# A three-stage fp32 kernel on one core: another order of instructions at the opening, at the entry of the value phase and in the last pair, and five more products on zeros

## The chip, the cores and the metric

The kernel runs on one core of a Trainium2 chip. The metric is the device time of one execution in microseconds (us); smaller is better. The engines of a core run side by side and meet at semaphores: TensorE (PE) multiplies, VectorE (DVE), ScalarE (ACT) and GpSimd (POOL) do the element-wise work, SyncE (SP) issues the DMAs.

## The reference

1024 tokens of width 512 pass through three blocks, each with a layer normalisation in front and a residual around it:

```python
x = x + 0.5 * ffn(layernorm(x))      # ffn: scores = xf @ Wr.T; top 16 of 64 experts, softmax gates G
x = x +       attn(layernorm(x))     #      h = xf @ A (64 experts of rank 16); out = (h * G) @ B * 2
x = x + 0.5 * ffn(layernorm(x))      # attn: q, k, v of 32 heads of 128, causal over 256 tokens, then wo
```

All of it is fp32. The mixture of low-rank experts is dense: up to 64 + 1024 columns for each token (the router's scores and all experts' h), gates that are zero for 48 experts, and down from 1024 to 512.

## The kernel before, in words

Every fp32 product is made of three products of a rounded part (hi) and a rest (lo): `mm3`, lines 226 to 229, whose instructions the profile shows as L227, L228 and L229. So whatever TensorE multiplies must first be split: one engine makes hi by a copy (ScalarE, L499), another makes lo by a subtraction (VectorE, L741 or L1523; GpSimd, L1291, L1073, L1014).

Tokens are worked on in 8 tiles of 128. For one tile the first feed-forward does this: VectorE takes mean and variance (`dve_stats`, L746, L748), GpSimd the reciprocal root (`pool_rstd`, L1005, L1008), VectorE normalises into `xn` (`dve_normalise`, L754), TensorE transposes xn in four pieces (`pe_ffn_transpose`, L235), ScalarE and VectorE split it into `xT_hi` and `xT_lo` (`act_ffn_transposed`, `dve_ffn_transposed`), TensorE multiplies by the up weights in three chunks of 384, 384 and 320 columns over four k (`pe_ffn_up`, PSUM banks `ub`), VectorE finds the top 16 and the gates (`dve_route`, L815 to L822) and writes the gated hidden values `hg` in three pieces (L830), TensorE transposes them in eight pieces (`pe_ffn_gated_transpose`, L268), they are split into `hT_hi` and `hT_lo`, TensorE multiplies by the down weights in 24 products of 512 columns (`pe_ffn_down`, bank `fb`), and VectorE adds the result to x (`dve_combine`, L845). TensorE's written order interleaves the tiles: gated transposes of t-1, up of t, transposes of t+1, down of t-1. `xT_hi` and `xT_lo` exist once.

For the first tile the order is by k, not by chunk (`pe_ffn_up_first`, L238), because the four slices of the up weights arrive by DMA one after the other and are split as they arrive (ScalarE L1440, VectorE L1523). Ahead of it stand ten products on zeros (L1342). GpSimd makes `downT_lo` in four subtractions (L1291) after the reciprocal root of tile 1 and ahead of that of tile 2.

The value phase makes v for all heads by a Strassen-like scheme with seven products per group and four groups: `pe_v(g, i, c)` is product i for column tile c of 128 tokens, six matrix instructions of 512 columns each. Its weights pass through a ring of three: ScalarE writes hi (`act_v_weight`), GpSimd the rest (`pool_v_weight`, L1073). Its inputs are the attention's normalised tokens `xa`, transposed (`pe_att_transpose`, L292), for tiles 4 to 7 with seven steps on VectorE that form the sums `comb_raw` (`dve_att_transposed_half1`, L779 to L791, counted by `comb_step`), a rounded copy on ScalarE (`act_combined`) and the rest on VectorE (`dve_combined`, counted by `comb_split`). The entry to this phase is interleaved with the last tiles of the feed-forward, lines 1370 to 1390 on TensorE.

Then come 16 pairs of heads. `pe_pair` has four steps j for a pair; step j holds products for the next pair's q and k, output products of earlier attention (`pe_output(p, t)`: tile t of x gets the pair's contribution, six instructions of 512 columns; VectorE adds it to x in `dve_output`, L939), transposes of the probabilities (`pe_prob_transpose`, L423), the scores of the next step (`pe_scores`, from L413) and the attended values (`pe_attend`, L441). Between scores and the next transposes lie VectorE's row maximum (L858), ScalarE's exponentials (L544), VectorE's reciprocal and scaling (L866, L870); between the transposes and the scores that overwrite their bank lie ScalarE's copies and VectorE's `pT_lo`. In the last pair (`final=True`) there are no q and k products of a next pair. After it come the transposes of the first tile of the second feed-forward, which is like the first, and the output products 2 to 7 of the last pair (lines 1414 to 1418).

All order is written out by hand, engine by engine; each engine works strictly in its written order and waits on semaphores. DMAs are issued by SyncE alone, in one queue.

## Time and profile before

| | us |
|---|---|
| median of 3 runs | 1074.53 |
| lowest, highest | 1071.37, 1075.76 |
| the profiled execution's own time | 1073.46 |
| its span, first to last instruction | 1071.5 |
| PE busy (share of the span) | 1048.3 (98%) |
| DVE busy | 693.1 (65%) |
| POOL busy | 511.2 (48%) |
| ACT busy | 481.9 (45%) |

Busy times are from one profiled execution. Engines overlap, so the shares don't add up. A busy TensorE is not one at its peak: its products are pipelined, and its granted clock has two levels, shown as a share of 2.4 GHz. The chain that ended last follows the work back from the last instruction to what released it each time.

### The profile page before, as it was taken

What the parts mean: (1) busy time and instruction counts of PE and PEld (TensorE: products, weight loads), DVE (VectorE), ACT (ScalarE), POOL (GpSimd) and SP (SyncE); (2) the same over time, 40 slices, a digit from 0 to 9 for tenths busy, and PEclk for the clock granted to TensorE, in tenths of its full rate; (3) what the DMA queues carried; (4) which work ended last, traced back from release to release, by engine and by line L of the source; (5) the groups of instructions that cost most, each with busy time, mean ns of one, the idle gap of its engine ahead of it and who ended that gap; (6) DMA issues with size and microseconds to landing.
All of it is one profiled execution on the core that took longest, in us unless ns stands there. A gap on an engine that the chain in (4) does not pass through costs nothing.

```text
span 1071.5 us, 18633 instructions
## 1 busy us (share of the span) xinstructions
PE 1048.3 (98%) x5652; PEld 907.5 (85%) x5652; DVE 693.1 (65%) x1888; ACT 481.9 (45%) x1387; POOL 511.2 (48%) x443
## 2 busy tenths in 40 slices
PE   7999999999999999999999999999999999989998
PEld 7999778888778888888888888888888888869997
DVE  6778842433467777767677677676776776866552
ACT  4112355554365555545455555555455555521110
POOL 5331268995267547446365474474564652210000
PEclk8999999999999999999999999999999999999999
DMA  9700235672623213123122222131231221450000
GB/s 365 316 0 1 108 142 202 238 269 93 226 65 93 71 51 98 51 84 98 49 88 69 78 88 65 53 101 46 88 90 56 88 69 57 156 218 11 20 20 30
DMA packets 48910, 110.11 MB, mean 103 GB/s; under 512 B 5360, under 2 KB 21744, under 8 KB 47344
## 3 DMA queue, kind: packets, MB, share of 16 engines
q1 hardware_dynamic: 48880, 109.73, 29.7%
q8 instruction: 16, 0.26, 0.1%
q14 instruction: 14, 0.11, 0.0%
HBM read 73.79 MB, written 35.91 MB: 102 GB/s over the span
## 4 chain that ended last, share of the span: by engine, by line
PE 93%; DVE 4%; ACT 1%; issue 1%; POOL 1%; DMA 1%; SPq 0%; DVEq 0%; POOLq 0%; ACTq 0%
PE bank L227 27%; PE bank L229 27%; PE bank L228 27%; PE bank L423 4%; PE bank L413 3%; PE bank L441 2%; PE bank L268 1%; DMA upT_raw<-up_w 1%; PE bank L235 1%; PE bank L292 0%; DVE xn L754 0%; DVE prob L870 0%; DVE st L746 0%; DVE xc_lo L741 0%; DVE pT_lo L741 0%
## 5 line engine op out<-in xcount | busy, mean ns | idle before, releaser
L544 ACT ACTIVATE bank<-bank,nmax 128x128 f32<-128x128 f32 (+1 forms) x256 | 101.4, 397 | 92.7 <-DVE nmax L858 92.7
L1030 POOL TENSOR_TENSOR stage_w<-stage_w 128x256 f32<-128x256 f32 x128 | 91.6, 737 | 89.8 <-DMA stage_w<-wqk 87.3
L939 DVE TENSOR_TENSOR x<-bank,x 128x512 f32<-128x512 f32 x128 | 87.8, 687 | 41.0 <-PE bank L229 41.0
L858 DVE CUSTOM_DVE_ANT_0 bank<-bank,mask 128x128 f32<-128x128 f32 (+1 forms) x256 | 83.4, 387 | 35.9 <-PE bank L229 35.9
L227 PE MATMUL bank<-wo_lo,attT_hi 128*128 128x512 f32 x256 | 100.4, 392 | 1.3 <-POOL wo_lo L1014 1.3
L229 PE MATMUL bank<-wo_hi,attT_hi 128*128 128x512 f32 x256 | 100.2, 391 | 0.0
L228 PE MATMUL bank<-wo_hi,attT_lo 128*128 128x512 f32 x256 | 99.6, 389 | 0.0
L870 DVE TENSOR_SCALAR prob<-bank,rinv 128x128 f32<-128x128 f32 (+1 forms) x256 | 95.0, 413 | 4.5
L1012 POOL CAST wq_hi<-stage_w 128x256 fp32r<-128x256 f32 (+1 forms) x31 | 28.4, 916 | 145.1 <-PE bank L229 145.1
L227 PE MATMUL bank<-xc_lo,wq_hi 128*128 128x512 f32 x224 | 94.7, 423 | 0.7 <-ACT s7q L499 0.7
L227 PE MATMUL bank<-xc_lo,wk_hi 128*128 128x512 f32 x224 | 92.4, 412 | 1.8 <-DVE s7k L898 1.5
L227 PE MATMUL bank<-ring,xc_hi 128*128 128x512 f32 x224 | 87.7, 391 | 2.8 <-ACT xc_hi L499 1.3
L229 PE MATMUL bank<-xc_hi,wq_hi 128*128 128x512 f32 x224 | 88.1, 393 | 0.0
L229 PE MATMUL bank<-xc_hi,wk_hi 128*128 128x512 f32 x224 | 87.9, 392 | 0.0
L228 PE MATMUL bank<-xc_hi,wq_lo 128*128 128x512 f32 x224 | 87.5, 391 | 0.0
L228 PE MATMUL bank<-xc_hi,wk_lo 128*128 128x512 f32 x224 | 87.2, 389 | 0.0
L229 PE MATMUL bank<-ring,xc_hi 128*128 128x512 f32 x224 | 87.2, 389 | 0.0
L228 PE MATMUL bank<-ring,xc_lo 128*128 128x512 f32 x224 | 87.2, 389 | 0.0
L1005 POOL TENSOR_SCALAR ve<-mv 128x1 f32<-128x1 f32 x24 | 5.5, 230 | 159.3 <-DVE mv L748 159.0
L1073 POOL TENSOR_TENSOR ring<-stage_v,ring 128x1024 fp32r<-128x1024 f32 x26 | 62.3, 2398 | 28.6 <-ACT ring L499 18.4
L227 PE MATMUL bank<-upT_lo,xT_hi 128*128 128x384 f32 (+1 forms) x192 | 64.9, 338 | 2.7 <-DVE xT_lo L741 2.7
L499 ACT COPY pT_raw<-bank 128x128 f32<-128x128 f32 x128 | 35.1, 275 | 70.2 <-PE bank L423 70.2
(144 smaller groups left out, 2979.5 us busy)
## 6 DMA issues: line engine op xcount, KB each, us to landing
stage_w<-wqk SPq DMA_DIRECT2D x32, 512.0 KB, 3.5
keep_v<-out_hl SPq DMA_DIRECT2D x64, 256.0 KB, 2.3
v<-keep_v SPq DMA_DIRECT2D x64, 256.0 KB, 2.8
stage_v<-wv SPq DMA_DIRECT2D x4, 2048.0 KB, 8.6
stage_wo<-wo SPq DMA_DIRECT2D x16, 512.0 KB, 3.3
keep_vraw<-out_raw SPq DMA_DIRECT2D x64, 128.0 KB, 2.1
v_raw<-keep_vraw SPq DMA_DIRECT2D x64, 128.0 KB, 3.1
upT_raw<-up_w SPq DMA_DIRECT2D x4, 544.0 KB, 6.5
```

Of the source, the lines that this page charges most:

```text
L227: nc.tensor.matmul(dst, a_hi, b_lo, start=first, stop=False, skip_group_check=onto)
L228: nc.tensor.matmul(dst, a_lo, b_hi, start=False, stop=False, skip_group_check=onto)
L229: return nc.tensor.matmul(dst, a_hi, b_hi, start=False, stop=last, skip_group_check=onto)
L413: nc.tensor.matmul(sp[b][:, 0:P], raw["q"][:, j, b * P:(b + 1) * P], raw["k"][:, j, b * P:(b + 1) * P], start=True, stop=True)
L423: last = nc.tensor.transpose(sp[b][:, i * P:(i + 1) * P], prob[:, b, i * P:(i + 1) * P], ident[:])
L499: return nc.scalar.copy(dst, src)
L544: nc.scalar.activation(sp[b][:, a:e], sp[b][:, a:e], ACT.Exp, bias=nmax[:, c:c + 1], scale=-1.0, accum_out=rsum[:, c:c + 1]).then_inc(s["e ...
L858: nc.vector.tensor_tensor_reduce(out=sp[b][:, a:e], in0=sp[b][:, a:e], in1=mask[:, a:e], scale=-SCALE, scalar=BIG, op0=ALU.add, op1=ALU.mi ...
L870: nc.vector.tensor_scalar(prob[:, b, a:e], sp[b][:, a:e], rinv[:, c:c + 1], None, ALU.mult).then_inc(s["p_ready"], 1)
L939: nc.vector.tensor_tensor(x[:, t, :], fp[t % 2][:, :], x[:, t, :], ALU.add).then_inc(s["fill_done"], 1)
L1030: nc.gpsimd.tensor_tensor(stage_w[:, out, :], stage_w[:, a, :], stage_w[:, b, :], op).then_inc(s["w_sum_s"], 1)
L1073: nc.gpsimd.tensor_tensor(r[:, 1, :, :], stage_v[min(g, 1)][:, V_WEIGHT[i], :, :], r[:, 0, :, :].bitcast(F32), ALU.subtract).then_inc(s["v ...
```

## The change

No computation is taken out. TensorE gets five more products on zeros; some instructions are cut in two; the rest is order, waits, and places in memory.

Opening. The first slice of the up weights is split in two parts (`FIRST`), the transposed first tile between them, and `up_split` counts to 5. Behind the transposes of the first tile stand five more products on zeros (`AGAIN`). The transposes of tile 1 stand ahead of the last k of the first tile's up products; tile 1 has its own `xT1_hi` and `xT1_lo`, and its up products (`pe_ffn_up_second`) stand in part ahead of the gated transposes of tile 0, in other banks (`ub2`). The down products of tile 0 go to `ub[0]`, and the up products of tile 2 wait for the combination of tile 0. GpSimd's four `downT_lo` subtractions wait for the normalisation of tile 1.

Entry of the value phase. The transposes of tile 7 stand ahead of the second product, and the engines' orders follow; the third weight's split on GpSimd waits for the third `comb_split` and is made in two slices, the fourth weight's waits for `comb_step` 24, where before the fourth waited for the fourth `comb_split` and the third for nothing but its copy.

Last pair. The second output of steps 0 and 1 stands behind the probability transposes; VectorE's row maximum stands ahead of the second output; outputs 2 and 3 stand ahead of the transposes of the next feed-forward; VectorE's normalisation of its first tile stands behind the last attended tile.

```diff
+AGAIN = 5
+FIRST = ((0, 384), (384, UPW))
+        xT1_hi = place("xT1_hi", [P, KD, P], F32R, at=where["s1"])
+        xT1_lo = place("xT1_lo", [P, KD, P], F32R, at=where["xa"])
+        ub2 = [lb, fb, ub[2]]
...
             for k in range(KD):
-                pe.wait_ge(s["up_split"], k + 1)
+                if k == KD - 1:
+                    pe_ffn_transpose(pe, 1)
                 for c, (a, b) in enumerate(CHUNKS):
+                    if c == 0:
+                        pe.wait_ge(s["up_split"], k + 1 if k == 0 else k + 2)
+                    elif k == 0 and c == 1:
+                        pe.wait_ge(s["up_split"], 2)
...
+        def pe_ffn_up_second(pe, c):
+            pe.wait_ge(s["xT_split"], 2)
+            a, b = CHUNKS[c]
+            if c == 2:
+                pe.wait_ge(s["hg_ready"], 3)
+            for k in range(KD):
+                last = mm3(ub2[c][:, 0:b - a], xT1_hi[:, k, :], xT1_lo[:, k, :],
+                           upT_hi[:, k, a:b], upT_lo[:, k, a:b], k == 0, k == KD - 1)
+            last.then_inc(s["up_ready"], 1)
...
@@ pe_pair @@
-                    if j < 2:
+                    if j < 2 and not final:
                         pe_output(pe, po, tb_)
                 pe_prob_transpose(pe, u)
...
-                if out and j >= 2:
+                if out and (j >= 2 or final):
                     pe_output(pe, po, tb_)
...
@@ dve_pair @@
-                    if j < 2:
+                    if j < 2 and not final:
                         dve_output(dve, po, tb_)
                 dve_prob_transposed(dve, u)
...
-                if out and j >= 2:
+                if final and j < 3:
+                    dve_softmax_max(dve, u + 1)
+                if out and (j >= 2 or final):
                     dve_output(dve, po, tb_)
                 if final and j == 3:
                     dve.wait_ge(s["fill_done"], 8 * p + 1)
                     dve_stats(dve, NT, 0, x[:, 0, :])
-                    dve_normalise(dve, NT, 0, x[:, 0, :])
-                else:
+                elif not final:
                     dve_softmax_max(dve, u + 1)
             if final:
                 dve_attended(dve, p, 3)
+                dve_normalise(dve, NT, 0, x[:, 0, :])
...
@@ pool_v_phase @@
-                    if VOPS * g + j == 1:
-                        pool.wait_ge(s["comb_split"], TH)
-                    if VOPS * g + j + 2 < VOPS * GROUPS:
+                    if VOPS * g + j == 0:
+                        pool.wait_ge(s["comb_split"], TH - 1)
+                        pool_v_weight(pool, 2, slices=2)
+                    elif VOPS * g + j == 1:
+                        pool.wait_ge(s["comb_step"], 6 * TH)
+                        pool_v_weight(pool, 3)
+                    elif VOPS * g + j + 2 < VOPS * GROUPS:
                         pool_v_weight(pool, VOPS * g + j + 2)
...
@@ GpSimd, opening @@
             pool_rstd(pool, 1, 0)
+            pool.wait_ge(s["xn_ready"], 2)
             for c in range(DC):
                 pool.wait_ge(s["down_hi"], c + 1)
...
@@ TensorE @@
             pe_ffn_transpose(pe, 0)
+            for _ in range(AGAIN):
+                nc.tensor.matmul(lb[:, 0:P], xa[:, 0:P], xa[:, 0:P], start=True, stop=True)
 
             pe_ffn_up_first(pe)
-            pe_ffn_transpose(pe, 1)
-
+            pe_ffn_up_second(pe, 0)
+            pe_ffn_up_second(pe, 1)
             pe_ffn_gated_transpose(pe, 0)
-            pe_ffn_up(pe, 1)
+            pe_ffn_up_second(pe, 2)
             pe_ffn_transpose(pe, 2)
-            pe_ffn_down(pe, 0, first=True)
+            pe_ffn_down(pe, 0, dst=ub[0], first=True)
 
             pe_ffn_gated_transpose(pe, 1)
+            pe.wait_ge(s["combined"], 1)
             pe_ffn_up(pe, 2)
...
             pe_v(pe, 0, 0, 3)
+            pe_att_transpose(pe, NT - 1, dst=vyz[3])
             pe_v(pe, 0, 1, 0)
             pe.wait_ge(s["combined"], NT)
             pe_v(pe, 0, 1, 1)
-            pe_att_transpose(pe, NT - 1, dst=vyz[3])
             pe_v(pe, 0, 1, 2)
...
             pe_pair(pe, PAIRS - 1, final=True)
+            for t in (2, 3):
+                pe_output(pe, PAIRS - 1, t)
             pe_ffn_transpose(pe, NT)
             pe.wait_ge(s["av_split"], 4 * PAIRS)
-            for t in range(2, NT):
+            for t in range(4, NT):
                 pe_output(pe, PAIRS - 1, t)
...
@@ ScalarE @@
-            for k in range(KD):
+            act.wait_ge(up_loaded[0], 16)
+            for part in range(2):
+                a, b = FIRST[part]
+                act_copy(upT_hi[:, 0, a:b], upT_raw[:, 0, a:b]).then_inc(s["up_hi"], 1)
+                if part == 0:
+                    act_ffn_transposed(act, 0)
+            for k in range(1, KD):
                 act.wait_ge(up_loaded[k], 16)
                 act_copy(upT_hi[:, k, :], upT_raw[:, k, :]).then_inc(s["up_hi"], 1)
-                if k == 0:
-                    act_ffn_transposed(act, 0)
             act_down_hi(act, 0)
+            act_ffn_transposed(act, 1, xT1_hi)
             act_down_hi(act, 1)
             act_gate_exp(act, 0)
-            act_ffn_transposed(act, 1)
...
+            act_att_transposed_half1(act, NT - 1, src=vyz[3])
+            act_v_weight(act, 3)
             act_v_high(act, 0, 0, 0)
-            act_att_transposed_half1(act, NT - 1, src=vyz[3])
+            act_combined(act, NT - 1)
             act_v_high(act, 0, 0, 2)
-            act_combined(act, NT - 1)
-            act_v_weight(act, 3)
...
@@ VectorE @@
+            dve_normalise(dve, 1, 0, x[:, 1, :])
+            dve_ffn_transposed(dve, 1, xT1_hi, xT1_lo)
...
-            step(0, 0, att=False, early=True, stats=False)
+            step(0, 0, att=False, early=True, stats=False, opening=True)
             dve.wait_ge(s["xr_loaded"], 16)
-            step(1, 1, att=False)
+            step(1, 1, att=False, src=ub2, down=ub[0])
...
             dve_v_sum(dve, 0, 0, 0)
+            dve_att_transposed_half1(dve, NT - 1)
             dve_v_sum(dve, 0, 0, 1)
             dve_v_low(dve, 0, 0, 0)
-            dve_att_transposed_half1(dve, NT - 1)
+            dve_combined(dve, NT - 1)
             dve_v_sum(dve, 0, 0, 2)
             dve_v_sum(dve, 0, 0, 3)
             dve_v_low(dve, 0, 0, 2)
-            dve_combined(dve, NT - 1)
...
             dve_pair(dve, PAIRS - 1, final=True)
+            dve_output(dve, PAIRS - 1, 2)
+            dve_output(dve, PAIRS - 1, 3)
             dve_ffn_transposed(dve, NT)
-            for t in range(2, NT):
+            for t in range(4, NT):
                 dve_output(dve, PAIRS - 1, t)
```

With `opening=True` VectorE's `step` leaves out the normalisation and the split of the next tile, which stand above it now.

## Rows read from the trace of the kernel before

**Rows 1.** The profile's page: chain that ended last by engine; one costly group.

```profile
PE 93%; DVE 4%; ACT 1%; issue 1%; POOL 1%; DMA 1%; SPq 0%; DVEq 0%; POOLq 0%; ACTq 0%
...
L939 DVE TENSOR_TENSOR x<-bank,x 128x512 f32<-128x512 f32 x128 | 87.8, 687 | 41.0 <-PE bank L229 41.0
```

**Rows 2.** Windows: stretch, length; PE, PEld, DVE, ACT, POOL busy; granted clock; DMA.

```profile
8.65:12.30 3.65, 3.65 (x13) 3.65 (x14) 3.31 (x5) 2.42 (x3) 0.00 (x0) 0.55 1.02 366
...
19.75:22.60 2.85, 2.85 (x12) 2.67 (x13) 2.81 (x7) 1.62 (x3) 2.85 (x2) 0.50 1.06 453
```

**Rows 3.** Timeline of PE, opening: start, us, engine, line, operation, shape [idle before].

```profile
8.65 0.44 PE L227 MATMUL bank<-upT_lo,xT_hi 128*128 128x384 f32 x1 [2.18 <-DVE xT_lo L741]
...
19.75 2.01 PE L268 MATMUL bank<-ident,hg 128*128 128x128 f32 x8 [2.16 <-DVE hg L830]
...
24.14 0.33 PE L227 MATMUL bank<-upT_lo,xT_hi 128*128 128x384 f32 x1
...
26.22 0.31 PE L227 MATMUL bank<-upT_lo,xT_hi 128*128 128x320 f32 x1
...
27.98 0.60 PE L235 MATMUL bank<-ident,xn 128*128 128x128 f32 x4
...
33.89 1.03 PE L268 MATMUL bank<-ident,hg 128*128 128x128 f32 x8
34.68 0.42 PE L227 MATMUL bank<-upT_lo,xT_hi 128*128 128x384 f32 x1
```

**Rows 4.** Timeline, opening: GpSimd's subtractions, VectorE's normalisations and combine.

```profile
14.18 4.89 POOL L1291 TENSOR_TENSOR downT_lo<-downT_raw,downT_hi 128x1024 fp32r<-128x1024 f32 x2
14.25 2.62 DVE L754 TENSOR_SCALAR xn<-x,mv,rstd 128x512 f32<-128x512 f32 x1 [0.72 <-POOL rstd L1008]
...
19.33 4.72 POOL L1291 TENSOR_TENSOR downT_lo<-downT_raw,downT_hi 128x1024 fp32r<-128x1024 f32 x2 [0.26 <-ACT downT_hi L499]
...
24.99 0.55 DVE L754 TENSOR_SCALAR xn<-x,mv,rstd 128x512 f32<-128x512 f32 x1 [1.79 <-POOL rstd L1008]
...
34.09 0.75 DVE L845 SCALAR_TENSOR_TENSOR x<-bank,ginv,x 128x512 f32<-128x512 f32 x1 [4.17 <-PE bank L229]
```

**Rows 5.** Timeline of PE, entry of the value phase.

```profile
131.39 0.50 PE L227 MATMUL bank<-ring,xc_hi 128*128 128x512 f32 x1 [1.29 <-ACT xc_hi L499]
...
137.81 0.50 PE L227 MATMUL bank<-ring,xc_hi 128*128 128x512 f32 x1 [0.69 <-DVE xc_lo L741]
...
140.28 0.51 PE L227 MATMUL bank<-ring,xc_hi 128*128 128x512 f32 x1 [0.81 <-POOL ring L1073]
```

**Rows 6.** Timelines of DVE and POOL, entry of the value phase.

```profile
125.39 2.60 DVE L754 TENSOR_SCALAR xa<-x,mv,rstd 128x512 f32<-128x512 f32 x1 [0.95 <-POOL rstd L1008]
...
131.37 0.43 DVE L779 TENSOR_TENSOR comb_raw<-half_raw,xc_hi 128x256 f32<-128x256 f32 x1 [0.29 <-ACT xc_hi L499]
...
133.90 0.42 DVE L791 TENSOR_TENSOR comb_raw<-comb_raw,xc_lo 128x256 f32<-128x256 f32 x1
...
125.32 2.39 POOL L1073 TENSOR_TENSOR ring<-stage_v,ring 128x1024 fp32r<-128x1024 f32 x1
137.83 7.11 POOL L1073 TENSOR_TENSOR ring<-stage_v,ring 128x1024 fp32r<-128x1024 f32 x3 [10.12 <-DVE xc_lo L741]
```

**Rows 7.** Timelines of PE and DVE, last pair.

```profile
930.92 0.49 PE L413 MATMUL bank<-kT_raw,qT_raw 128*128 128x128 f32 x2 [1.21 <-DVE pT_lo L741]
...
943.21 0.55 PE L423 MATMUL bank<-ident,prob 128*128 128x128 f32 x3 [0.74 <-DVE prob L870]
...
948.75 0.50 PE L227 MATMUL bank<-wo_lo,attT_hi 128*128 128x512 f32 x1 [1.27 <-POOL wo_lo L1014]
...
955.61 0.66 PE L235 MATMUL bank<-ident,xn 128*128 128x128 f32 x4 [2.01 <-DVE xn L754]
...
947.50 0.17 DVE L866 RECIPROCAL rinv<-rsum 128x2 f32<-128x2 f32 x1 [0.35 <-ACT bank L544]
...
956.92 0.69 DVE L741 TENSOR_TENSOR xT_lo<-bank,xT_hi 128x512 fp32r<-128x512 f32 x1 [0.77 <-ACT xT_hi L499]
```

More of the change, by code:

```diff
@@ L503, in act_down_hi, with act_ffn_transposed @@
             act_copy(down_chunk(downT_hi, c), down_chunk(downT_raw, c)).then_inc(s["down_hi"], 1)
-        def act_ffn_transposed(act, n):
+        def act_ffn_transposed(act, n, xT_hi=xT_hi):
             act.wait_ge(s["xT_ready"], n + 1)
@@ L755, in dve_normalise, with dve_ffn_transposed @@
                                     ALU.subtract, ALU.mult).then_inc(done, 1)
-        def dve_ffn_transposed(dve, n):
+        def dve_ffn_transposed(dve, n, xT_hi=xT_hi, xT_lo=xT_lo):
             dve.wait_ge(s["xT_hi_done"], n + 1)
@@ L804, in dve_gated_transposed, with dve_route @@
                    hT_hi[:, 4 * i:4 * i + 4, :].rearrange("p k t -> p (k t)")).then_inc(s["hT_split"], 1)
-        def dve_route(dve, n):
+        def dve_route(dve, n, ub=ub):
             step = [5 * n]
@@ L1066, in pool_v_sum, with pool_v_weight @@
             last.then_inc(s["v_weight_sum"], 1)
-        def pool_v_weight(pool, n):
+        def pool_v_weight(pool, n, slices=1):
             g, i = n // VOPS, n % VOPS
@@ L1072, in pool_v_weight @@
             r = ring[n % SLOTS]
-            nc.gpsimd.tensor_tensor(r[:, 1, :, :], stage_v[min(g, 1)][:, V_WEIGHT[i], :, :],
-                                    r[:, 0, :, :].bitcast(F32), ALU.subtract).then_inc(s["v_weight_split"], 1)
+            step = 2 // slices
+            for k in range(0, 2, step):
+                last = nc.gpsimd.tensor_tensor(r[:, 1, k:k + step, :], stage_v[min(g, 1)][:, V_WEIGHT[i], k:k + step, :],
+                                               r[:, 0, k:k + step, :].bitcast(F32), ALU.subtract)
+            last.then_inc(s["v_weight_split"], 1)
         def pool_v_first(pool, n):
@@ L1228, in _ @@
             load_wo(sync, 0)
-            sync.wait_ge(s["up_split"], KD)
+            sync.wait_ge(s["up_split"], KD + 1)
             for i, t in enumerate((upT_hi, upT_lo)):
@@ L1293, in _ @@
                                         ALU.subtract).then_inc(s["down_split"], 1)
-            pool.wait_ge(s["up_split"], KD)
+            pool.wait_ge(s["up_split"], KD + 1)
             pool_rstd(pool, 2, 0)
@@ L1520, in _ @@
             dve_normalise(dve, 0, 0, x[:, 0, :])
-            for k in range(KD):
-                dve.wait_ge(s["up_hi"], k + 1)
+            for part, (a, b) in enumerate(FIRST):
+                dve.wait_ge(s["up_hi"], part + 1)
+                nc.vector.tensor_tensor(upT_lo[:, 0, a:b], upT_raw[:, 0, a:b], upT_hi[:, 0, a:b].bitcast(F32),
+                                        ALU.subtract).then_inc(s["up_split"], 1)
+                if part == 0:
+                    dve_ffn_transposed(dve, 0)
+            for k in range(1, KD):
+                dve.wait_ge(s["up_hi"], k + 2)
                 nc.vector.tensor_tensor(upT_lo[:, k, :], upT_raw[:, k, :], upT_hi[:, k, :].bitcast(F32),
                                         ALU.subtract).then_inc(s["up_split"], 1)
-                if k == 0:
-                    dve_ffn_transposed(dve, 0)
                 if k == KD - 2:
@@ L1529, in _, with step @@
                     dve_stats(dve, 1, 0, x[:, 1, :])
-            def step(t, n, att=True, last=False, early=False, stats=True, half1=False, combined=None):
+            dve_normalise(dve, 1, 0, x[:, 1, :])
+            dve_ffn_transposed(dve, 1, xT1_hi, xT1_lo)
+            def step(t, n, att=True, last=False, early=False, stats=True, half1=False, combined=None, opening=False,
+                     src=ub, down=fb):
                 if not last and stats:
@@ L1539, in step @@
                     dve_combined(dve, combined)
-                if not last:
+                if not last and not opening:
                     dve_normalise(dve, n + 1, 0, xt(t + 1))
@@ L1543, in step @@
                     dve_normalise(dve, t - 2, 1, xt(t - 2))
-                dve_route(dve, n)
-                if not last:
+                dve_route(dve, n, src)
+                if not last and not opening:
                     dve_ffn_transposed(dve, n + 1)
@@ L1551, in step @@
                 if not early:
-                    dve_combine(dve, n - 1, t - 1)
+                    dve_combine(dve, n - 1, t - 1, down)
             def stats_after(t):
```

## The prediction

> **What bounds the kernel now.** First the chain that ended last, by engine: 93% of it is TensorE's own work [rows 1], so inside its steady stages an order can gain nothing. Time can come back only where TensorE stands still or runs at its lower clock. The second view is therefore that chain in order of time, to find the pieces that are not TensorE; then TensorE's timeline there; then that of the engine it waits for. The holes lie in three places. In the opening TensorE idles 2.2 us before the first token tile's products and 2.2 us before its gated transposes [rows 3], and each hole is followed by a stretch at a granted clock of 0.55 and 0.50, so 1.2 and not 2.4 GHz [rows 2]. At the entry of the value phase it stops three times inside 11 us [rows 5]. In the last pair it waits twice for split probabilities (the second wait is like the one shown), once for a probability half, once for wo, and once for the normalisation of the next feed-forward [rows 7]. The profiled execution took 1073.46 us, its span 1071.5 and 2.0 around it; the sum below is made against it. The median of the runs shown, 1074.53, lies 1.07 above, and I carry that over.
>
> **Opening.** Prices at full clock [rows 3]: 12 products of 384 columns 2.08 us (24.14 to 26.22), 12 of 320 columns 1.76, hence one of the four k steps of a tile a quarter of 2.08 + 2.08 + 1.76, 1.48; eight transposes 0.79; four transposes with 24 products of 512 columns 5.91, so 0.23 a product.
> Splitting the first k in two lets TensorE begin some 0.8 before 8.65, at 7.9. This gains nothing by itself, for the loads of the later k come as before, and what ends this stretch next is the added wait: tile 1's transposes now stand before k = 3. From 7.9 three k steps take 4.4 at full clock; with load waits they end at about 13.3, after a stretch at half clock at 14.8. The normalisation of tile 1 began at 14.25 and took 2.62, because GpSimd's subtraction had started at 14.18; the third tile's, with nothing beside it, took 0.55 [rows 4]. GpSimd now waits for it, so xn is there at 14.8 in either case. Transposes from 14.86, k = 3 from 15.3 to 16.9. From the start of such transposes to the end of the split is 2.0 (955.61 to 956.92 plus 0.69) [rows 7]: 16.9 too, so tile 1's products follow with no gap. Two chunks, 24 products, end at 21.05. Routing of tile 0 starts as now; its gate operation can stand behind a subtraction of GpSimd that lies 0.7 later, so the first gated piece, at 19.7 now (it released the 19.75 row [rows 3]), comes at 20.5 at the latest, covered by those chunks. Gated transposes to 21.85, last chunk to 23.6. Now that point is 27.98.
> The five products on zeros are ten passes. They lie between the first transposes (6.4) and 7.9 and fill most of the hole; if they run slow they end near 8.6, before the later k are loaded, and cost nothing. All that they can give is the clock of k = 0 to 2, which the wait to 14.8 swallows either way.
> Late next is the normalisation of tile 2. Its rstd stands on GpSimd's queue behind the four downT_lo subtractions, 4.89 and 4.72 for two each [rows 4], 9.6 in all. They began at 14.18 and ended at 24.05, with xn following at 24.99 to 25.54. They now begin at 14.85, and end at 24.45; xn is ready at 25.9. TensorE, free at 23.6, waits 2.3, and queued behind its transposes are tile 0's down products and all that follows. From 25.95 these 5.91 end at 31.9, the next gated transposes at 32.7. The down sum now sits in the bank that the next up products need, so they wait for VectorE's combine, 0.2 + 0.75 behind the last product (34.09 against 33.89 [rows 3, 4]): they start at 32.95, against 34.68. Gain 1.7 at full clock.
> The clock takes some of it. Both waits of this size in the opening were followed by low clock, 2.85 us of the second one's shown at 0.50 [rows 2]; the 2.01 us before the last transposes was not, the granted clock staying 1.00 there. A drop behind the new wait costs up to 1.7, so the opening yields between nothing and 1.7, and up to 2.7 where the executions before fared worse than their profile. I take 0.9, the middle of the two ends that this trace knows.
>
> **Entry of the value phase.** Idle 1.29, 0.69 and 0.81 with a restart of some 0.15 behind each [rows 5]: 3.3 us. The root is tile 7's normalisation, 2.60 from 125.39, beside GpSimd's ring subtraction from 125.32 [rows 6]. That subtraction now waits for the third comb_split, so the normalisation takes 0.55 and ends at 125.94. The transposes move ahead of the second product, to 125.3, wait 0.7 there (cover gone; price included), and the second product runs from 126.6 over its four column tiles, 1.37 each, to 132.1; three of the next, to 136.2. ACT's two copies after the transposes end by 127.9, so no wait for them. VectorE's seven steps take 2.95 (131.37 to 134.32) [rows 6]. They follow one sum that ends at 128.65, and their first stands behind GpSimd's subtraction, now in two slices from 127.1 to about 129.85: end 132.7. This releases GpSimd's next subtraction, 2.37 (a third of 7.11 [rows 6]), ready at 135.1 and wanted at 137.6, and ACT's cast of 1.05, then VectorE's split of tile 7, 1.1 long. The split starts free at 133.9 or, behind that subtraction, at 135.1; the end is 135.1 or 136.25, and TensorE wants it at 136.2. The fourth product starts at 137.65, against 140.28: gain 2.6. If each of the last steps slips one more GpSimd operation the gain is 1.3 less; if nothing collides, 0.4 more: 1.3 to 3.0.
> The row shows VectorE's operation ending at 127.99, just behind GpSimd's at 127.71: one blocks the other, they don't share [rows 6]. The Trainium skill (SBUF — State Buffer, Who interferes with whom) states it as an exclusive lock for a whole instruction, which VectorE also takes with two SBUF inputs. By that rule, and the trace agrees for the normalisation, the split ends at 136.25; were it not to hold for the split, 135.1, and the gain 2.7.
>
> **Last pair.** For j = 0 and 1 the second output moves behind the probability transposes. TensorE meets the second probability half earlier and waits there, but the stop of 1.21 idle before the scores [rows 7] is then filled by products: scores 0.25 earlier. VectorE's output moves behind the maximum, 0.69 long [rows 1] in an idle gap of 0.35 [rows 7], so it delays each following step by 0.2 and all three together come out 0.26 earlier: this chain is VectorE's and ACT's, and filling TensorE's holes shortens it little. The wait for wo, 1.27 [rows 7], begins with output 7 and stays. At the end outputs 2 and 3, 12 products or 2.75 us, go in front of the transposes and cover their wait, 2.01 of idle and 0.4 around it [rows 7]; their inputs are halves split long before. VectorE splits the last attended tile in GpSimd's rstd gap and not after, so outputs 4 to 7 don't wait. 0.3 + 2.4 = 2.7. If fill_done of a moved output comes late, one output step (0.69) is lost: 1.8 to 3.1.
>
> **Sum.** 0.9 + 2.6 + 2.7 = 6.2: 1073.46 − 6.2 = 1067.3 for an execution like the profiled one, 1074.53 − 6.2 = 1068.3 for the median.
>
> **Rivals.** (a) The clock stays up: opening 1.7 to 2.7, time 1066.5 to 1067.5. For it, the zeros fill one hole; against it, the wait of 2.3. (b) The entry's collisions come in series on GpSimd: 1.3 there and 0 to 0.9 in the opening, in all 4.0 to 4.9, time 1069.6 to 1070.5. For it, GpSimd starts its third ring split 1.8 later; against it, 2.5 us of slack before the fourth product. (c) The zeros don't hold the clock: the wait to 14.8 swallows it, 1068.3 all the same. (d) Slower: GpSimd's chain of the opening, hidden until 27.98 now, becomes the path of the whole start, and stretches. The change loses when that chain ends 6.2 later than I have it, at 30.7: 4.0 a subtraction for 2.4. At 4.5 each the time is 1076.7. Against it, two of them beside the whole routing took 4.72 [rows 4].
>
> **Chances.** Forecast with (c) 0.50, (a) 0.24, (b) 0.23, (d) 0.03. A measurement here tells 0.5%, 5.4 us, from no change: the line is 1069.2. The forecast lies only 0.9 below it, with runs before from 1071.37 to 1075.76, so a fifth of it falls to same: faster 0.64, same 0.33, slower 0.03. The range 1065.3 to 1071.0 takes in (a) with both upper ends of the later stages and (b) whole.
>
> **What would show it.** Right: the second xn and the last xa at 0.55; TensorE's transposes of tile 2 at 25.9, behind GpSimd's rstd; low clock after them or not decides between forecast and (a); the fourth value product 2.6 closer to the last down product; the transposes after the last pair without a wait. Wrong: downT_lo over 2.5 each (d), a wait of over 1 us for comb_split (b), over 0.5 before the last transposes, or a gain of one stage handed back by the next.

## The result, and the profile after

| | before | after |
|---|---|---|
| median of the timed executions | 1074.2 us (1071.4 to 1076.4, 6 executions beside it) | 1065.85 us (1065.5 to 1067.2, 6) |
| ratio, 95% interval | 1 | 0.9928 [0.9912, 0.9944] |
| profiled execution, its span | 1073.46, 1071.5 | 1066.8, 1064.7 |
| mean granted clock of that execution | 0.996 | 0.998 |

The change makes the kernel 8.35 us faster, 0.7%; the forecast was 6.2. The executions of the changed kernel fall into two groups: four with a mean granted clock of 1.000 and spans of 1063.4 to 1063.8, two with 0.998 and spans of 1064.7 and 1065.1. A stretch in which the granted clock falls to its lower level is called a drop below; the second group has one. The profiled one is of the second group, so it lies 1 above the median where the one before lay 0.7 below; of the 8.35 the two profiles show 6.7.

The chain that ended last, by engine, answers to [rows 1]:

```profile
PE 94%; DVE 3%; POOL 1%; ACT 1%; issue 1%; DMA 0%; POOLq 0%; DVEq 0%; ACTq 0%
```

Windows of the opening (stretch, length; PE, PEld, DVE, ACT, POOL busy; granted clock; DMA share, GB/s) answer to [rows 2]:

```profile
5.80:8.00 2.20, 1.83 (x15) 1.67 (x15) 1.33 (x3) 1.45 (x3) 0.65 (x2) 1.00 1.01 398
8.00:10.00 2.00, 1.91 (x9) 1.35 (x9) 1.89 (x2) 2.00 (x3) 0.00 (x0) 1.00 1.02 361
19.75:22.60 2.85, 2.85 (x23) 2.82 (x22) 2.31 (x6) 0.97 (x2) 2.85 (x2) 1.00 1.06 448
22.60:26.00 3.40, 1.48 (x12) 1.22 (x11) 1.88 (x6) 0.11 (x1) 2.30 (x3) 1.00 0.97 401
26.00:29.50 3.50, 3.50 (x13) 2.74 (x12) 3.09 (x13) 0.82 (x2) 0.00 (x0) 0.55 1.08 461
```

The low clock of the first products is gone, and that of the first gated transposes; a new stretch at 0.55 stands behind the wait for tile 2.

TensorE's timeline in the opening (start, length, line, operation, idle before and its releaser) answers to [rows 3]:

```profile
6.35 1.28 PE L1378 MATMUL bank<-xa 128*128 128x128 f32 x10
7.92 0.44 PE L233 MATMUL bank<-upT_lo,xT_hi 128*128 128x384 f32 x1 [0.28 <-DVE xT_lo L763]
14.66 0.66 PE L241 MATMUL bank<-ident,xn 128*128 128x128 f32 x4 [1.20 <-DVE xn L776]
21.00 1.03 PE L290 MATMUL bank<-ident,hg 128*128 128x128 f32 x8
25.70 0.66 PE L241 MATMUL bank<-ident,xn 128*128 128x128 f32 x4 [1.92 <-DVE xn L776]
34.28 0.44 PE L233 MATMUL bank<-upT_lo,xT_hi 128*128 128x384 f32 x1
```

The 6.35 row is the products on zeros. First products start at 7.92 (8.65 before), the gated transposes at 21.00 without a wait, tile 2's transposes at 25.70, and its up products at 34.28 (34.68 before).

The engines that TensorE waits for there, VectorE and GpSimd, answer to [rows 4]:

```profile
14.06 0.55 DVE L776 TENSOR_SCALAR xn<-x,mv,rstd 128x512 f32<-128x512 f32 x1 [0.72 <-POOL rstd L1032]
14.69 9.46 POOL L1323 TENSOR_TENSOR downT_lo<-downT_raw,downT_hi 128x1024 fp32r<-128x1024 f32 x4 [0.66 <-DVE xn L776]
24.51 0.55 POOL L1032 TENSOR_TENSOR rstd<-ve,half_neg 128x1 f32<-128x1 f32 x1
25.10 0.55 DVE L776 TENSOR_SCALAR xn<-x,mv,rstd 128x512 f32<-128x512 f32 x1 [1.49 <-POOL rstd L1032]
```

Tile 1's normalisation takes 0.55 instead of 2.62. GpSimd's four subtractions run from 14.69 and tile 2's rstd follows on their heels: the path that the forecast named.

TensorE's timeline at the entry of the value phase, answering to [rows 5], and VectorE's and GpSimd's, answering to [rows 6]:

```profile
125.60 0.66 PE L314 MATMUL bank<-ident,xa 128*128 128x128 f32 x4 [0.57 <-DVE xa L776]
126.02 0.47 PE L233 MATMUL bank<-ring,xc_hi 128*128 128x512 f32 x1
135.75 0.50 PE L233 MATMUL bank<-ring,xc_hi 128*128 128x512 f32 x1
137.26 0.39 PE L233 MATMUL bank<-ring,xc_hi 128*128 128x512 f32 x1
125.00 0.55 DVE L776 TENSOR_SCALAR xa<-x,mv,rstd 128x512 f32<-128x512 f32 x1 [0.95 <-POOL rstd L1032]
133.25 2.45 DVE L763 TENSOR_TENSOR xc_lo<-comb_raw,xc_hi 128x1024 fp32r<-128x1024 f32 x1
132.20 2.41 POOL L1099 TENSOR_TENSOR ring<-stage_v,ring 128x1024 fp32r<-128x1024 f32 x1 [2.89 <-DVE comb_raw L813]
```

TensorE now waits once, 0.57. The fourth value product starts at 137.26, 3.02 earlier; the stage began 0.39 earlier (xa at 125.00 against 125.39), so 2.63 are its own. GpSimd's subtraction from 132.20 takes its usual 2.41, to 134.61; VectorE's split, issued beside it at 133.25, takes 2.45 and ends at 135.70, 1.09 behind the subtraction. The subtraction held the split up, and not the other way round. TensorE goes on at 135.75.

TensorE's and VectorE's timeline in the last pair answers to [rows 7]:

```profile
926.93 0.38 PE L435 MATMUL bank<-kT_raw,qT_raw 128*128 128x128 f32 x2
931.98 0.55 PE L445 MATMUL bank<-ident,prob 128*128 128x128 f32 x3 [0.86 <-DVE prob L892]
944.33 0.50 PE L233 MATMUL bank<-wo_lo,attT_hi 128*128 128x512 f32 x1 [1.28 <-POOL wo_lo L1038]
951.79 0.60 PE L241 MATMUL bank<-ident,xn 128*128 128x128 f32 x4
952.15 0.48 PE L233 MATMUL bank<-wo_lo,attT_hi 128*128 128x512 f32 x1
965.66 0.45 PE L233 MATMUL bank<-upT_lo,xT_hi 128*128 128x384 f32 x1 [0.53 <-DVE xT_lo L763]
```

The same point as this last row, the first up product of the second feed-forward, in the kernel before:

```profile
972.47 0.45 PE L227 MATMUL bank<-upT_lo,xT_hi 128*128 128x384 f32 x1 [0.53 <-DVE xT_lo L741]
```

The stop of 1.21 before the scores is gone, one of 0.86 to 0.88 before the second probability half stands in its place (three times), and the last transposes run without a wait. The product behind the wait for wo comes 4.42 earlier (944.33 against 948.75), the first up product of the second feed-forward 6.81 earlier (965.66 against 972.47).

### The profile page after: what moved, and what is told of

It reads as the page before. It is cut to its first block, busy times and chain, and to the rows that moved or that the text cites. A ratio compares the mean times of both kernels' runs of the same rounds, so it can differ in the third digit from the quotient of the medians.

```text
span 1064.7 us, 18660 instructions
## 1 busy us (share of the span) xinstructions
PE 1047.4 (98%) x5662; PEld 906.3 (85%) x5662; DVE 691.5 (65%) x1889; ACT 482.4 (45%) x1388; POOL 512.0 (48%) x444
## 4 chain that ended last, share of the span: by engine, by line
PE 94%; DVE 3%; POOL 1%; ACT 1%; issue 1%; DMA 0%; POOLq 0%; DVEq 0%; ACTq 0%
PE bank L233 28%; PE bank L235 28%; PE bank L234 27%; PE bank L445 4%; PE bank L435 3%; PE bank L463 3%; PE bank L290 1%; POOL downT_lo L1323 1%; PE bank L241 1%; DVE prob L892 0%; PE bank L314 0%; DVE st L768 0%; DVE bank L880 0%; DVE upT_lo L1570 0%; DMA x<-x_in 0%
## 5 line engine op out<-in xcount | busy, mean ns | idle before, releaser
L1099 POOL TENSOR_TENSOR ring<-stage_v,ring 128x1024 fp32r<-128x1024 f32 (+1 forms) x27 | 62.7, 2322 | 25.4 <-ACT ring L521 20.7
L763 DVE TENSOR_TENSOR pT_lo<-bank,pT_hi 128x256 fp32r<-128x256 f32 x128 | 54.4, 425 | 19.6 <-ACT pT_hi L521 18.4
```

Of the source, the lines that this page charges most:

```text
L763: return nc.vector.tensor_tensor(dst, src, hi.bitcast(F32), ALU.subtract)
L1099: last = nc.gpsimd.tensor_tensor(r[:, 1, k:k + step, :], stage_v[min(g, 1)][:, V_WEIGHT[i], k:k + step, :], r[:, 0, k:k + step, :].bitcast ...
```

## The experiments

**One part of the change at a time.** Three kernels, e1 to e3, each the one before with the edits of one place. Their medians stand against one median before of 1074.2.

The opening alone (e1: tile 1's transposes and up products ahead, GpSimd's wait, the zeros):

```diff
+                if k == KD - 1:
+                    pe_ffn_transpose(pe, 1)
...
+            pool.wait_ge(s["xn_ready"], 2)
```

> The kernel before with the opening's edits alone. Theory (my ledger of the two profiles): the opening starts tile 2's up products 0.4 us earlier when the clock drops behind the wait for tile 2's normalisation, about 1.7 earlier when it does not, and four of six executions of the changed kernel were at a mean granted clock of 1.000. So the median is 1.2 to 2.2 us below the kernel before, executions with a drop 1.3 above those without. Rival: the zeros and the early first products give more than the trace of one execution shows, 2.7 or more. Rival: the opening's gain is nothing by itself, and the excess over my sum comes from an interplay with the later stages: 0 to 0.5.

Measured: 1073.23 (12 executions), ratio 0.9993 [0.9981, 1.0004], not to be told from no change. By mean clock, three executions at 1.000 have spans of 1069.3 to 1069.4, four at 0.998 have 1070.6 to 1071.3, five at 0.996 have 1071.9 to 1072.4. The kernel before, 24 executions, never reached 1.000: 1069.4 to 1071.3 at 0.998, to 1074.3 at 0.993. So the fastest executions of the two kernels are alike (1069.3 and 1069.4), and the 1.0 between the medians, under the 1.2 expected, comes from the longer ones. That the opening gains anything by itself is not shown by the times.

The entry alone (e2):

```diff
+            pe_att_transpose(pe, NT - 1, dst=vyz[3])
             pe_v(pe, 0, 1, 0)
...
+                        pool.wait_ge(s["comb_split"], TH - 1)
+                        pool_v_weight(pool, 2, slices=2)
```

> The kernel before with the edits at the entry of the value phase alone. Theory: 2.6 us off the median, in the profile 2.6 less from the first value product to the fourth. Rival: part of the gain needs the shifted opening; then 2.0 or less. If the three single parts add up to less than 7 us, the changed kernel's 8.35 below before is more than the sum, and the rest has to be found elsewhere.

Measured: 1069.71 (1068.7 to 1073.8), 0.9961 [0.9947, 0.9974]. In its profile the fourth value product comes 12.23 behind the start of tile 7's normalisation, where it was 14.89 before (140.28 against 125.39): 2.66, as expected. The profiled execution is its slowest, and says why the times spread. Here are its window in the opening, TensorE's row at the last transposes, and the windows before and behind that row.

```profile
19.60:26.40 6.80, 6.14 (x22) 5.97 (x23) 4.83 (x13) 2.28 (x4) 5.45 (x4) 0.50 1.00 420
```

```profile
954.39 0.73 PE L235 MATMUL bank<-ident,xn 128*128 128x128 f32 x4 [2.01 <-DVE xn L754]
```

```profile
950.00:954.00 4.00, 2.38 (x16) 1.98 (x14) 2.54 (x6) 1.12 (x4) 0.74 (x2) 1.00 0.04 16
954.00:958.00 4.00, 3.61 (x11) 2.85 (x12) 1.67 (x4) 0.58 (x1) 0.00 (x0) 0.60 0.00 0
```

The wait is the 2.01 of [rows 7]. In the profile of before the clock behind it stayed 1.00, as in that of e1; here it falls to 0.60. From the product behind the wait for wo to the first up product of the second feed-forward TensorE now takes 25.25 where the kernel before took 23.72, so the drop costs 1.5. Another 2.1 was lost ahead of the entry, whose normalisation starts at 127.49 and not at 125.39: this execution's low clock in the opening lasted longer than that of [rows 2].

The last pair alone (e3):

```diff
-                    if j < 2:
+                    if j < 2 and not final:
...
-                if out and j >= 2:
+                if final and j < 3:
+                    dve_softmax_max(dve, u + 1)
+                if out and (j >= 2 or final):
...
+            for t in (2, 3):
+                pe_output(pe, PAIRS - 1, t)
             pe_ffn_transpose(pe, NT)
```

> The kernel before with the edits of the last pair alone. Theory (ledger): 3.2 us, of which 0.7 within the four steps of the pair (I had forecast 0.3) and 2.5 at the transposes of the next feed-forward. Rival: the steps give only 0.3 and the whole is 2.7; the 0.7 seen was a difference between two executions.

Measured: 1070.01 (1069.3 to 1071.6), 0.9963 [0.9950, 0.9975]. In its profile the stretch from the scores of j = 0 to the wo product is 24.26, against 24.95 before, and from there to the first up product of the second feed-forward 21.32 against 23.72: 0.69 and 2.40, together 3.1. The rival, 0.3 for the steps, falls. The three medians give 1.0 + 4.5 + 4.2 = 9.7 where all together give 8.35. Intervals of 0.2 to 0.3% on each leave room for that; nothing says that the parts help or hinder each other.

**The zeros (e4).**

```diff
-AGAIN = 5
+AGAIN = 0
```

> The changed kernel without its five additional products on zeros. Theory: TensorE has k = 0 to 2 at half clock in most executions; k = 2 then ends near 14 to 15 and the wait for the second tile's normalisation (14.7 in the changed kernel) swallows it: 0 to +0.5 us, and the mean granted clock falls to about 0.998 or 0.996. Rival: the zeros are what keeps the whole opening at full clock; without them also the stretch of k = 3 and of tile 1's chunks runs at half, +1.3 to +2.

Measured: 1067.14 (1065.3 to 1067.4), 0.9933 [0.9915, 0.9952]. The windows of its opening, and TensorE's row at tile 1's transposes:

```profile
5.80:8.00 2.20, 0.63 (x4) 0.42 (x4) 1.33 (x3) 1.24 (x3) 0.86 (x2) 1.00 0.98 338
8.00:12.30 4.30, 4.18 (x14) 3.77 (x15) 4.13 (x6) 3.24 (x4) 0.00 (x0) 0.60 1.02 375
```

```profile
14.98 0.66 PE L241 MATMUL bank<-ident,xn 128*128 128x128 f32 x4 [0.38 <-DVE xn L776]
```

The zeros do hold the clock (1.00 against 0.60 from 8.00), so rival (c)'s reason is wrong; its other half is right, since the wait before tile 1's transposes shrinks from 1.20 to 0.38 and takes most of the loss (they start 0.3 later, 14.98 against 14.66, where the other profiles with the zeros and GpSimd's wait have 14.63 to 15.50; and what follows waits for GpSimd, tile 2's up products starting at 33.00). The fastest spans, 1063.2 and 1063.4, are no longer than the changed kernel's fastest, 1063.4; one drop in this place costs nothing that can be seen. The medians lie 1.3 apart with overlapping intervals, and the pair of kernels at the end of this section, 0.1 apart, says the same: no gain from the zeros.

**GpSimd's order in the opening.** First (e5) tile 2's rstd, the root of the new wait, taken ahead of the last downT_lo subtraction:

```diff
+                if c == DC - 1:
+                    pool_rstd(pool, 2, 0)
...
-            pool_rstd(pool, 2, 0)
```

> The changed kernel with GpSimd's reciprocal root of token tile 2 ahead of the last of the four downT_lo subtractions instead of behind it. Theory (the opening is bound by this queue): TensorE's 1.9 us wait in front of tile 2's transposes shrinks to 0.5 or less, tile 2's up products start 1.4 to 1.9 earlier, and no execution has low clock behind that wait: 1.5 us off executions without a drop, 2.8 off those with one; median 1064.2 or a little below. Rival: the down products then wait for the last subtraction, which is 0.8 later, and take the gain back: 0 to 0.5.

Measured: 1065.41 (1065.0 to 1065.6), 0.9918 [0.9902, 0.9934], mean clock 1.000 in all executions. The wait shrank less than expected, from 1.92 to 1.62. VectorE's, GpSimd's and TensorE's rows:

```profile
24.03 1.83 DVE L776 TENSOR_SCALAR xn<-x,mv,rstd 128x512 f32<-128x512 f32 x1
23.21 2.37 POOL L1325 TENSOR_TENSOR downT_lo<-downT_raw,downT_hi 128x1024 fp32r<-128x1024 f32 x1
25.91 0.66 PE L241 MATMUL bank<-ident,xn 128*128 128x128 f32 x4 [1.62 <-DVE xn L776]
```

The normalisation starts 1.1 earlier (24.03 against 25.10) but takes 1.83 instead of 0.55: it ends at 25.86, just behind the subtraction that moved in beside it (25.58). I had cost only the queue, not the blocking. (The Trainium skill, SBUF — State Buffer, Who interferes with whom, states this as an exclusive lock for a whole instruction; the trace agrees, 1.83 against 0.55.) Tile 2's up products start at 32.90, no earlier than in an execution with the changed kernel's own opening and no drop (32.84, shown at e8 below), though here the first products start 0.24 later. At equal clock the spans, 1062.9 to 1063.5, lie some 0.3 below the changed kernel's; the rest of the difference is that six executions of six are at 1.000, for four of six. With the subtraction held until the normalisation is done (e11):

```diff
+                    pool_rstd(pool, 2, 0)
+                    pool.wait_ge(s["xn_ready"], 3)
```

> The reciprocal root of tile 2 ahead of the last subtraction, which now also waits for tile 2's normalisation. With the root alone moved, the normalisation began 1.1 us earlier but took 1.83, blocked by that subtraction, and TensorE still waited 1.6. Theory: now it takes 0.55, TensorE waits 0.4 and tile 2's up products start 1.3 us earlier than with the root alone moved: median near 1064.0, all executions without a drop. Rival: the down products then wait for the last part of downT_lo, which ends near 27.2: 0 to 0.3 gained.

Measured: 1064.07 (1063.9 to 1064.9), 0.9905 [0.9885, 0.9925], mean clock 1.000 in all executions. TensorE's rows at tile 2, and the window there:

```profile
24.75 0.66 PE L241 MATMUL bank<-ident,xn 128*128 128x128 f32 x4 [0.32 <-DVE xn L776]
31.73 0.44 PE L233 MATMUL bank<-upT_lo,xT_hi 128*128 128x384 f32 x1
```

```profile
22.00:27.00 5.00, 4.68 (x31) 4.11 (x29) 4.24 (x15) 1.90 (x4) 3.36 (x4) 1.00 1.02 425
```

The wait is 0.32, the clock stays up, and tile 2's up products start at 31.73, for 32.90 with the root alone moved and 34.28 in the changed kernel's profile with its drop.

The other way round (e6): without the change's own wait, which keeps tile 1's normalisation free.

```diff
-            pool.wait_ge(s["xn_ready"], 2)
```

> The changed kernel in which GpSimd's downT_lo subtractions no longer wait for the normalisation of token tile 1. Theory: xn of tile 1 takes 2.6 us beside the first subtraction, k = 3 and tile 1's chunks come 2.1 later, but GpSimd's queue starts 0.5 earlier and still sets the transposes of tile 2, so of the 2.1 only what exceeds the 1.9 us wait shows: -0.4 to +0.3 us, and fewer executions with a drop of the clock, since TensorE's wait there is nearly gone; another opens earlier. Rival: everything behind xn moves by 2.1, +2.

Measured: 1068.25 (1067.4 to 1069.1), 0.9946 [0.9927, 0.9964], 2.4 above the changed kernel. My expectation fell, the rival's held.

```profile
16.94 0.66 PE L241 MATMUL bank<-ident,xn 128*128 128x128 f32 x4 [3.23 <-DVE xn L776]
14.33 2.55 DVE L776 TENSOR_SCALAR xn<-x,mv,rstd 128x512 f32<-128x512 f32 x1 [0.72 <-POOL rstd L1032]
19.25 7.08 POOL L1322 TENSOR_TENSOR downT_lo<-downT_raw,downT_hi 128x1024 fp32r<-128x1024 f32 x3 [2.64 <-ACT downT_hi L521]
27.88 0.66 PE L241 MATMUL bank<-ident,xn 128*128 128x128 f32 x4 [0.42 <-DVE xn L776]
```

The blocked normalisation (2.55) makes TensorE's transposes late, ScalarE's copy of them too, and behind that copy in ScalarE's queue stands the downT_hi copy that GpSimd's second subtraction needs. So GpSimd loses more than the head start gave it, and tile 2's transposes come at 27.88 instead of 25.70. Fewer drops were expected too, and more came: all six executions have mean clocks of 0.997 or 0.998, and in the profile the clock is low behind the wait of 3.23. So the 2.4 holds some clock as well; against e8's profile, whose opening has no drop, tile 2's transposes and up products both come 2.04 later.

**The entry's added wait (e7).** The third weight's split free again, whole, beside the normalisation:

```diff
-                        pool.wait_ge(s["comb_split"], TH - 1)
-                        pool_v_weight(pool, 2, slices=2)
+                        pool_v_weight(pool, 2)
```

> The changed kernel in which the third weight's split on GpSimd waits for nothing but its copy again and is one operation; the moved transposes and everything else stay. Theory (one engine blocks the other on the port): xa is again 2.5 us long, the transposes, now ahead of the second product, wait 2 us longer, and the value phase's fourth product comes 1.7 to 2.2 later: +2 us. Rival: the gain of this stage came from the place of the transposes, not from GpSimd's wait; then +0.5 or less.

Measured: 1068.84 (1067.2 to 1070.9), 0.9948 [0.9928, 0.9967], 3.0 above the changed kernel. Executions at clock 1.000 have spans of 1065.1 to 1065.2, 1.5 above the changed kernel's at that clock; those at 0.996 and 0.997, 1068.2 to 1068.8. The profiled one is of these:

```profile
127.98 0.66 PE L314 MATMUL bank<-ident,xa 128*128 128x128 f32 x4 [2.58 <-DVE xa L776]
```

```profile
125.00:129.00 4.00, 1.42 (x8) 0.88 (x7) 3.63 (x2) 0.91 (x2) 2.65 (x2) 0.98 1.01 426
129.00:133.00 4.00, 4.00 (x12) 3.22 (x11) 2.08 (x6) 2.28 (x4) 0.00 (x0) 0.59 0.07 29
```

The blocked normalisation costs 1.5 by itself, so of the stage's 2.63 about 1.1 is left for the place of the transposes. The rival, 0.5 or less, falls. Three of six executions are 3.0 to 3.7 longer again. The profiled one, 3.3 longer, has two drops: one in the opening behind the wait of 1.92, as in the changed kernel, and one to 0.59 behind the 2.58 us wait.

**The last pair's steps.** First (e8) the steps j = 0 to 2 in the old order, the products ahead of the last transposes kept:

```diff
-                    if j < 2 and not final:
+                    if j < 2:
...
-                if out and (j >= 2 or final):
+                if out and j >= 2:
```

> The changed kernel with steps j = 0 to 2 of the last pair in the old order; outputs 2 and 3 still stand ahead of the next transposes. Theory (ledger of two profiles): +0.7 us. Rival (my forecast): +0.26. A second rival: the old stops of 1.2 us sometimes bring a drop of the clock, so some executions are 1.5 longer and the median moves by 1 or more.

Measured: 1066.85 (1065.9 to 1068.3), 0.9935 [0.9918, 0.9952]. At clock 1.000 its spans are 1063.8 to 1063.9 against 1063.4 to 1063.8, some 0.3 longer; in its profile the stretch from the scores of j = 0 to the wo product is 24.94, as before (24.95), against 24.27. That stretch settles what the steps are worth: it is 24.93 to 24.95 in the four profiles with the old order (before, e1, e2, e8) and 24.26 to 24.29 in the seven with the new one (after, e3 to e7, e11), 0.67 to 0.69 less. Three of e8's executions, at 0.998, lie 0.9 to 1.0 above the changed kernel's two at that clock; where their drops stood is not on record, so the second rival stays open.

This profile also shows the changed kernel's opening without a drop:

```profile
25.84 0.66 PE L241 MATMUL bank<-ident,xn 128*128 128x128 f32 x4 [1.88 <-DVE xn L776]
32.84 0.44 PE L233 MATMUL bank<-upT_lo,xT_hi 128*128 128x384 f32 x1
```

```profile
26.00:29.50 3.50, 3.50 (x18) 2.95 (x18) 3.23 (x13) 0.82 (x2) 0.00 (x0) 1.00 1.07 459
```

From the transposes to the up products it takes 7.00, and 8.58 behind the drop in the changed kernel's profile: this drop costs 1.6.

Then (e9) the changed kernel with VectorE's output ahead of its maximum again:

```diff
-                if final and j < 3:
-                    dve_softmax_max(dve, u + 1)
                 if out and (j >= 2 or final):
                     dve_output(dve, po, tb_)
+                if final and j < 3:
+                    dve_softmax_max(dve, u + 1)
```

> The changed kernel with VectorE's second output of a step of the last pair ahead of the row maximum instead of behind it. VectorE idles 0.96 us in front of each maximum in the changed kernel's profile and the output ends the product 0.2 after the scores start, so theory: it fits there, the reciprocal is no longer delayed, and each of the steps is 0.1 shorter: -0.3 us in all, at the limit of what can be measured. Rival: it delays the maximum itself by up to 0.2 a step: +0.3.

Measured: 1066.21 (1065.2 to 1067.2), 0.9924 [0.9907, 0.9941]. The median lies above the changed kernel's, but it holds another mix of clocks; at 1.000 its spans are 1063.1 to 1063.4, 0.3 below. In the pair itself the profile shows half of that: from scores to scores the steps take 6.86, 6.75 and 6.74, for 6.87, 6.82 and 6.82 in the changed kernel, and the stretch to the wo product 24.11 for 24.27. The rival, +0.3, falls.

**The two together.** e11 with this swap (e12), and then the same without the zeros (e13):

```diff
+                    pool.wait_ge(s["xn_ready"], 3)
...
                     dve_output(dve, po, tb_)
+                if final and j < 3:
+                    dve_softmax_max(dve, u + 1)
```

> The same with VectorE's second output ahead of the row maximum in the last pair. Theory: the two parts add up, another 0.3: median near 1063.7. It would be the fastest so far. Rival: the swap's 0.3, seen between executions of the same clock, was chance: the same as with the first move.

Measured: 1063.79 (1063.6 to 1064.4), 0.9902 [0.9882, 0.9923].

```diff
-AGAIN = 5
+AGAIN = 0
```

> The same without the five additional products on zeros. The wait before tile 2's transposes, which could swallow a late opening, is now short, but the wait for tile 1's normalisation stands. Theory: k = 0 to 2 at half clock end at 14 to 15, swallowed there, unless the low stretch reaches into tile 1's chunks, which some executions do: median +0 to +1.0, mean clock 0.998 in most. Rival: the zeros are needed: +1.4 to +1.8 in every execution.

Measured: 1063.66 (1063.5 to 1064.0), 0.9902 [0.9882, 0.9923]. Both beat the kernel before by 10.4 to 10.6 and the changed one by 2.1 to 2.2; between them there is no difference. In e13 three executions have a mean clock of 0.998 and two 1.000, with the same spans, 1061.4 to 1061.9; in the profiled one the low clock lies at k = 0 to 2, where e4 has it.

## Why the prediction was nearly right, and which terms were mis-sized

- **Direction and mechanism: right.** The holes went where it said, and no stage handed a gain back. The median lies 2.45 below the forecast and 0.65 below the lower end given for rival (a), inside the stated range.
- **Opening, 0.9: the path is right.** The xn at 0.55, the transposes of tile 2 at 25.70 (25.9 said), the gated pieces without a wait, the drop behind the wait of 1.92. With the drop tile 2's up products come 0.40 earlier (34.68 to 34.28), without it 1.84 (32.84 in e8's profile, where 32.95 and 1.7 were said). Four of six executions have no drop and lie about 1.3 lower: in most, rival (a)'s clock is what happened. The 0.9 lies between these two.
- **Entry, 2.6: right to 0.1** in the profiles, 2.63 and 2.66. The split ended 1.1 behind the subtraction that held it, as said, at 135.70 (136.25 said, in a stage that then began 0.39 earlier).
- **Last pair, 2.7: 3.1 in the profiles.** The covered wait at the transposes is right, 2.39 for 2.4. The mis-sized term is the 0.26 for the steps: it is 0.68 (24.27 for 24.95). The first step gains 0.25, as said (6.87 for 7.12), but the second gains 0.41 (6.82 for 7.23), where a delay of 0.2 by VectorE's output behind the maximum was said to take most of it. That delay is what failed: taking it away, in e9, shortens each of the two following steps by 0.07 to 0.08. How the forecast's 0.26 comes out of 0.25 a step and 0.2 of delay is not written out in it.
- **What was missing is, as far as is known, in the clock.** The entry and the last pair alone give 4.5 and 4.2 in medians, where their profiles give 2.7 and 3.1. The forecast said that the 2.01 us before the last transposes kept the clock at 1.00: true of the one execution read, not of the kernel. e2 shows a drop at that very wait, which cost 1.5, and e7 one at the entry behind 2.58. The kernel before had mean clocks of 0.993 to 0.998, and a removed wait can take its share of drops with it. The forecast had carried the distance from profile to median, 1.07, over unchanged; but from fastest execution to fastest the gain is 5.9, from slowest to slowest 9.2, so what the medians add to the profiles' 6.7 lies mostly in the longest executions of before. That the clock makes this 1.7 is argued and not shown: how often each wait of before dropped it was not counted, as only one execution of a kernel has a timeline.
- **Luck.** The profiles' ledger is 0.40 + 2.63 + 3.07 = 6.1, and another 0.7 lies in stretches that the change does not touch, most of it in the 16 pairs: see the last section. The forecast's 6.2 meets the ledger partly by luck, +0.4 in the last pair against −0.5 in the opening.
- **Rivals.** (b) had its collision but it stayed under the slack; (c)'s reason fell, but its claim that the clock of k = 0 to 2 is worth nothing held; (d)'s subtractions took 9.46 for four, 2.4 each and not 4.5.

## What to carry to other kernels

Where a small operation of VectorE is the root of TensorE's wait, hold GpSimd's large subtraction behind it rather than let it start in the gap: at the three places tried this was worth 1.3 (e11 against e5, all at clock 1.000), 2.4 (e6, some of it the clock's) and 1.5 us (e7, at equal clock). Moving the root ahead in its queue isn't enough when this sets it beside such a subtraction. Cost a TensorE wait of some 2 us with a chance of low clock behind it, whatever the one profile shows: where nothing downstream covered it, the drop cost 1.5 to 1.6. For differences of a few tenths of a us compare the same stretch in many profiles; the mean granted clock of an execution helps only where its drops fall in the same place.

## What the hardware showed unexpectedly

Behind the same wait of 2.01 us the granted clock stayed at 1.00 in two profiles (before, e1) and fell to 0.60 in another (e2); behind the same wait of 1.9 us in the opening it fell to 0.55 in the changed kernel's profile and stayed at 1.00 in e8's. The mean clock of an execution does not tell what its drops cost: in the changed kernel one was worth 1.3, in e13 none of it shows, and e2's executions at 0.996 (1067.5 to 1067.7) are shorter than three of its four at 0.998 (1068.0 to 1068.5).

The steady pairs run at two paces. From the scores of one pair to those of the twelfth behind it took 506.40 us in the profiles of the kernel before, of the last pair alone and of e11, and 505.92 in all the others, 0.09% less, with nothing in the code or in the granted clock that would tell them apart. Over the 15 intervals from pair to pair that is 0.6 us. It fits that e11's profiled execution has a span of 1062.8 where its four others, also at 1.000, have 1061.7 to 1062.0; apart from it, the spans of one kernel at a mean clock of 1.000 lie within 0.6 of each other.
